# First edge layer: where in VectorE's turn the index copy, the row statistics and the scales of a batch stand

## The reference, cut to what matters

```
edge_index = stack([src, dst])                       # 2 x 25000
h   = maximum(layernorm(x), 0)                       # 50000 x 256
xt  = einsum('ni,rio->rno', h, weight)               # 8 relations, 256 x 256 each
out = segment_sum(xt[edge_type, dst], src)           # one row per edge, summed by node
x   = x + relu(out + bias)
```

## Time and profile before

| | us |
|---|---|
| median of 3 runs (lowest, highest) | 3427.87 (3419.07, 3433.84) |
| the profiled execution, its own time | 3424.89 |
| its span | 3423.2 |
| mean granted TensorE clock | 0.912 |
| VectorE busy over the span | 3036.0 (89%) |
| GpSimd busy | 2461.4 (72%) |
| TensorE matmul busy | 2528.3 (74%) |
| ScalarE busy | 2198.9 (64%) |

### The profile page before, as it was taken

The page is one execution under the profiler, slowest core; times in us unless marked ns, Lnnn a source line. Parts: engine busy times, 40 slices in busy tenths (PEclk is TensorE's granted clock), DMA queues, the critical chain, the costliest instruction groups (busy, mean ns, idle before and its releaser), DMA issues.

```text
span 3423.2 us, 64727 instructions
## 1 busy us (share of the span) xinstructions
PE 2528.3 (74%) x10740; PEld 1658.5 (48%) x10741; DVE 3036.0 (89%) x13368; ACT 2198.9 (64%) x6002; POOL 2461.4 (72%) x1732
## 2 busy tenths in 40 slices
PE   3665766767788888888777777777777775777787
PEld 1224655555566666666533333333333333565565
DVE  8999778888899999999789999999999997777777
ACT  5994233323333333333379999999999995777776
POOL 0004886767788888888678888888888885777775
PEclk8998888888899999999989999999999998999989
DMA  9702466666655555555544545445455453889897
GB/s 364 285 0 52 80 116 150 144 139 152 127 105 106 103 106 103 106 103 106 84 155 175 194 173 189 178 173 194 172 186 181 174 190 145 295 285 303 285 306 252
DMA packets 308089, 576.91 MB, mean 169 GB/s; under 512 B 32095, under 2 KB 188034, under 8 KB 307982
## 3 DMA queue, kind: packets, MB, share of 16 engines
q1 hardware_dynamic: 212366, 419.40, 35.9%
q0 software_dynamic: 95616, 156.31, 23.5%
HBM read 316.70 MB, written 258.88 MB: 168 GB/s over the span
## 4 chain that ended last, share of the span: by engine, by line
DVE 45%; issue 24%; PE 15%; DMA 7%; POOL 5%; DVEq 2%; ACT 1%; POOLq 1%; ACTq 0%; SPq 0%
DVE best L1165 6%; DVE w L1172 6%; DVE zone_c L1172 6%; PE banks L1574 5%; DMA agg<-msg,sidx 4%; PE banks L1474 4%; DMA w<-hs,gidx 2%; POOL w L734 2%; PE banks L1416 2%; DVE zone_c L846 2%; DVE zone_c L1050 2%; DVE zone_c L1054 2%; DVE zone_c L848 2%; DVE zone_c L1200 2%; DVE zone_c L1052 2%
## 5 line engine op out<-in xcount | busy, mean ns | idle before, releaser
L1546 PE MATMUL banks<-w,hT 128*128 128x512 f32 x1568 | 764.5, 645 | 252.2 <-ACT hT L1326 247.7
L667 POOL DMA_INDIRECT agg<-msg,sidx x400 | 667.1, 1668 | 185.2 <-issue 123.0
L655 POOL DMA_INDIRECT rows_in<-in_x,gidx x400 | 433.4, 1084 | 414.9 <-DVE gidx L871 280.5
L1546 PEld LDWEIGHTS banks<-w,hT 128*128 128x128 f32 x1568 | 312.8, 204 | 646.0 <-issue 508.7
L1200 DVE SCALAR_TENSOR_TENSOR zone_c<-banks,rdeg,zone_c 128x256 f32 x784 | 379.3, 484 | 158.6 <-PE banks L1574 123.1
L1574 PE MATMUL banks<-w,zone_c 128*128 x1568 | 405.5, 417 | 143.2 <-POOLq L742 113.8
L1416 PE MATMUL banks<-pick,h 128*128 128x128 f32 x1600 | 286.3, 307 | 301.1 <-ACT h L1217 206.1
L1474 PE MATMUL banks<-w,hT 128*128 x1600 | 482.7, 430 | 16.5 <-issue 15.1
L1235 ACT COPY msg<-banks 128x256 f32<-128x256 f32 x400 | 148.2, 370 | 510.9 <-PE banks L1485 486.5
L734 POOL DMA_INDIRECT w<-hs,gidx x392 | 372.5, 950 | 143.5 <-issue 93.8
L1416 PEld LDWEIGHTS banks<-pick,h 128*128 128x128 f32 x1600 | 256.1, 214 | 365.2 <-issue 343.1
(11 more groups left out here) (229 smaller groups left out, 5793.9 us busy)
## 6 DMA issues: line engine op xcount, KB each, us to landing
out_rows<-zone_c SPq DMA_DIRECT2D x196, 512.0 KB, 2.7
agg<-bias SPq DMA_DIRECT2D x2, 25344.0 KB, 97.4
zone_c<-agg SPq DMA_DIRECT2D x98, 512.0 KB, 6.1
hs<-zone_c SPq DMA_DIRECT2D x98, 512.0 KB, 3.6
zone_c<-out_rows SPq DMA_DIRECT2D x98, 512.0 KB, 5.9
rows_in<-in_x SPq DMA_DIRECT2D x97, 512.0 KB, 5.4
keyrow<-key_rows SPq DMA_DIRECT2D x100, 320.0 KB, 3.9
zone_c<-bucket_rows SPq DMA_DIRECT2D x28, 448.0 KB
```

What stands on the lines that cost most here:

```text
L655: pool.indirect_dma_start(out=rows_in[p][:, j, :], out_offset=None, in_=x[:, :], in_offset=bass.IndirectOffsetOnAxis(ap=gidx[p][:, j:j + 1 ...
L667: pool.indirect_dma_start(out=agg[:, :], out_offset=bass.IndirectOffsetOnAxis(ap=sidx[p][:, j:j + 1], axis=0), in_=msg[p][:, j * D:(j + 1) ...
L1546: last = mm(bank[4 + j][:, :], hT[p][:, c, j * P:(j + 1) * P], w1[:, c, :], start=(c == 0), stop=(c == KC - 1))
```

## The change

VectorE's part of a batch from the wait for the gathers on, with the index copy, the statistics and the scales, becomes a function of its own, and `edge0_body` calls it at the end of the turn, for the same batch b. The order of a turn was front with statistics and scales (b), cross and back (b-1), side work. It is now front (b), cross and back (b-1), side work, statistics and scales (b). No instruction is added or removed, and no other engine's program changes.

```
                 v.tensor_tensor(livekey[p][:, :], extra[p][:, :], keycol[p][:, :], ALU.add).then_inc(live0, 1)
+
+            def edge0_scales(b, r, p):
+
                 dve.wait_ge(gathered0[p], 16 * B * (r + 1))
                 v.tensor_copy(gidx[p][:, :], from0[:, bass.ds(b * B + 2 * B, B)]).then_inc(staged0, 1)
                 statistics(b, p, rows_in, stats0, var0)
-
                 scales(b, p, std0, recip0, rstd0)
...
                     sort_hots(c, rc, pc)
+                b, r, p = at.back(0)
+                if inside(b, NBT):
+                    edge0_scales(b, r, p)
 
             phased(dve, PHASES, 2, NBT, edge0_body)
```

## The result

The changed kernel takes 3659.82 us (median of 4 runs, 3654.23 to 3661.09) against 3427.88 for the kernel before; the ratio is 1.0674 [1.0652, 1.0697]. That is slower by 232 us, where +191 was forecast. It lies 0.2 us inside the upper end of the range (3530 to 3660), and above the forecast's own range, which ended at 3655.

The account below looks back on a forecast made before the run. VectorE, the busiest engine, was taken as the bound. 5 - 27 + 74 + 135 + 0 + 4 = +191 us on 3424.9 gives 3615.9, forecast as 3618; own range 3555 to 3655, 8-in-10 range 3530 to 3660.

Parts of the forecast that it names:

- part (2): VectorE's `cross` waits for TensorE's product 0: sort +135 us (bounds +77 to +157), rank +74 (+39 to +80).
- rival B: `edge0_back` waits for GpSimd's adds of two batches before, 1.5 us late in most turns: +42, 3660; chance 0.09.
- part (3): `cross`, `sidx` and side work come earlier on VectorE; the key row's 14.1 us wait goes; worth 0 or -14.
- If `back` waits for adds: Sign of being wrong: VectorE's `back` waits for GpSimd's adds in the changed kernel; no size given.
- rival A: TensorE's clock stays high, so `cross` waits only 1.4 us: +90, or 3518; chance 0.09.
- Part (1): The gather wait moves to the turn's end: -27 us in rank; +5 in turns 0 to 12, ends -10 and +20.
- Turns 41 to 43: These three turns lose 3.4 + 4.7 us of waits and gain 3 x 2.65: 0.
- The tail: Turn 99 and what follows it: +4 us, ends 0 and +8.
- D: The waits lie elsewhere, and gains and losses cancel within 0.5% (17 us); chance 0.02.
- C: Product 0 is there when VectorE reaches `cross`, so the gather and key waits go for nothing: 3361; chance 0.04.

Follow-up runs that it names:

- e3: Changed kernel, but only `cross` 3 waits for product 0, `cross` 0 to 2 for the products of batch b-2; 3658.13 us.
- e4: Changed kernel with 14 filler matmuls on constants at the end of each TensorE body of the sort turns; 3660.24 us.
- e5: Changed kernel, but ScalarE copies message 3 of a batch ahead of the front of the batch two on; ratio to the kernel before 1.0629.
- e6: Changed kernel with the edits of e5 and e3 together; ratio to the kernel before 1.0451.
- e7: Changed kernel with the edit of e5 and the filler matmuls of e4; ratio to the kernel before 1.0494.
- e2: Changed kernel, but `cross` and `back` stand behind the side work, just ahead of the moved block at the turn's end; 3478.52 us.
- e9: Changed kernel, but the gather wait and index copy stand in the front again, statistics and scales stay late; ratio to the kernel before 1.0618.
- e10: Changed kernel, but gather wait, index copy and statistics stand in the front again, only the scales stay late; ratio to the kernel before 1.0182.
- e1: Changed kernel, but the moved block stands behind `cross` and `back` and ahead of the side work; 3446.44 us.
- e8: The kernel before, but ScalarE copies message 3 ahead of the front, the edit of e5; ratio to the kernel before 1.0075.
- e11: Changed kernel, but the moved block stands between `cross` and `back`, ahead of the side work; ratio to the kernel before 0.9960.

## Why the prediction was right, and where it was short

**The chain from E to `cross`, part (2): right in mechanism and size.** Waits of 2.45 in 55 turns, 135 us, were forecast for sort; 134.0 were measured. For rank 74 were forecast and 69.9 measured. Product 0 came at E + 5.9 to 6.3 in 53 of the 55 sort turns, and the granted clock in sort fell. The choice of the low clock from the length of the pause held: TensorE's pauses in sort were 2.7 to 4.6 us (4.03 in the turn shown). That the wait came out to 1 us in 135 is partly luck. In the mean of the sort turns product 0 came at E + 6.13, 0.18 later than the 5.95 I took, and VectorE reached `cross` at E + 3.76, 0.26 later than the 3.50, since its turn starts late; the two nearly cancel.

**The step that failed is rival B and part (3).** I let GpSimd's adds start from message 0 and had them land at E + 22.7, half a microsecond ahead of their need: a loop of two turns. I missed that ScalarE's copy of message 3 stands behind the normalising, so that add 3 has a chain of its own, from E to `back` of the very next turn. Counted from the E one turn earlier, as B counts, add 3 is issued at 16.06 + 3.69 = 19.75 and lands at about 23.6. B had two slips: it missed message 3, and it counted the 3.8 us from the end of the issuing instruction, where the earlier trace rows counts them from its start. Without message 3 the add would by B's own terms start at 17.3 and land at 21.1, 2 us ahead of its need; message 3 takes these 2 us and makes the add the last to arrive. Measured: `met` waits 16.5 us in sort, 12.2 in rank (0.7 before), and 24.0 in turns 0 to 12, with single waits up to 8.3. I gave B 0.09; its wait came true beside the forecast, not in its place, and not by B's mechanism, a loop of two turns. "If `back` waits for adds" was one of my signs of being wrong, and it does in 53 of the 55 sort turns. That the time still lies in the range, and on B's 3660, is luck: the range reached so far up only to take in a B that works otherwise. e3 to e7 show that it also made the lower bound of (2) wrong: with chain 2 in place, neither a higher clock nor a shorter wait in `cross` gives the lower sum of rival A. In e4 the higher clock was tried, at 0.92, and gave nothing.

**What was put at zero and is not.** "Lowcol" has 15.5 us of issue in 35 turns, 0.46 each, at the first instruction of a loop iteration, and `pick` waits 7.1 us for `keycol`: with the block's waits at the end of the turn, VectorE's sequencer doesn't get ahead of the engine over the loop's start. The branch and the register work of the next iteration, hidden before, are bare. The trace shows it for the turn above: the loop's branch and register work (L86, L916) run from 1461.17 to 1461.65, between `shift` and the next copy. In the kernel before, the same branch runs at 1305.60 and the register work at 1306.03, over 2 us ahead of the copy that starts turn 71 at 1308.13, while VectorE still makes one-hots. The nine kernels whose turn ends with the block or with the scales (the changed kernel, e2 to e7, e9, e10) have the row, 34 or 35 times each; the four whose turn ends with side work (before, e1, e8, e11) don't. No run changed it alone. In sort it is 17.9 us, of the 24.5 by which the stretch missed the forecast; the adds are 16.5, and the 9.5 of `met` behind `cross`, which I hadn't counted as won, go off.

**Part (1) held.** The waits for gathers went; 27 in rank as forecast. In turns 0 to 12 they went too, but the time didn't: 24.0 of waits for adds came for 22.1 of waits for gathers, and 21.0 of waits for product 0 beside them; +14.3 measured, +5 taken, ends -10 and +20. I had let GpSimd's rate hide much of the new wait. e2 says otherwise: it has the same 24.0 for adds but 5.1 for product 0, and its turns 0 to 12 take 194.6 us, not 211.6. So here, too, it is the wait for product 0 that costs.

Turns 41 to 43: +3.4 for 0, with 5.5 us of waits for adds. The tail: +1.1 for +4. One slip in the sum: 3615.9 and 3.0 make 3619, not 3618.

**The rivals.** A and D did not occur. C, that product 0 would be there in time, is refuted by 98 waits. The Trainium skill ("Perfetto Trace Analysis", Optimization Strategy) says to find what the busiest engine's gaps wait for and make it start sooner. The change did remove those gaps (52.6 us of gathers), though by coming later to them and not by starting the gathers sooner, and VectorE's busy share fell from 89% to 83% nevertheless. So the advice isn't refuted here; it names the gaps there are, and the price was in a dependency that had next to no gap yet (one wait of 4.6 us).

## What to carry to other kernels

Before a producer is moved to the end of a loop's turn, list every consumer chain that starts at it and comes back to the same engine in the next turn, through every engine and its hand-written order, and add what stands between the end of the turn and each of them; here that was 3.5 us against two chains of 7.6. When two chains end within a few tenths of each other, cutting either one moves the wait and hardly the time, and only both cuts together show what each is worth. Place such a block where it fills an existing short wait and has the long work behind it: between `cross` and `back`, 0.4% were won with the same instructions.

## What the runs showed of the hardware

With a wait and two short instructions at the very end of a loop body, the next iteration's first instruction came about 0.45 us late on VectorE in 35 of 100 turns, with nothing waited for: a branch and register work of the sequencer stand in that time. The loops run two turns an iteration over 70 of the 100 turns, so this is every iteration; the 30 turns without a loop around them don't show it.

TensorE's granted clock in sort rose with filler work (0.85 to 0.92 in e4, 0.95 in e7, whose turns are shorter), yet this won time only where TensorE's chain was alone at the end. The length of the pause alone doesn't tell the clock: in e7, behind pauses of the same 1.70 us, product 0 came anywhere from E + 4.88 to E + 6.30. Behind the pauses of 2.7 us and more of the changed kernel's sort turns it never came before E + 5.36.

An add of GpSimd took 3.8 us from the start of its instruction to its landing, in the sort turn shown and in the tail.
